# Prologue of a windowed-attention kernel: load order, issuing engine, who makes the weights' high parts, and when a slab is measured

## The reference

```python
g = v.reshape(B, H, W, 32, 12)                     # group norm: 32 groups of 12 channels
xn = (g - mean(g, (1, 2, 4))) / sqrt(var(g) + eps) # statistics over a whole image
x_ = roll(xn, (-3, -3), axis=(1, 2))
q, k, v = split(x_ @ w_qkv.T, 3)                   # 12 heads of 32, windows of 7 x 7 tokens
dots = q @ k.T * 32**-0.5 + pos_emb[rel] + mask    # 49 x 49 for each window and head
out = softmax(dots) @ v
y = x + roll(out @ w_out.T + b_out, (3, 3), axis=(1, 2))
```

## Time and profile before

| | |
|---|---|
| median of 3 runs | 4351.02 us |
| the profiled execution | 4347.23 us, its span 4345.4 us |
| TensorE (PE) busy | 4176.7 us, 96% |
| VectorE (DVE) busy | 3730.7 us, 86% |
| ScalarE (ACT) busy | 2266.6 us, 52% |
| GpSimd (POOL) busy | 2231.0 us, 51% |

### The profile page before, as it was taken

The page is one execution under the profiler, slowest core; times in us unless marked ns, Lnnn a source line. Parts: engine busy times, 40 slices in busy tenths (PEclk is TensorE's granted clock), DMA queues, the critical chain, the costliest instruction groups (busy, mean ns, idle before and its releaser), DMA issues.

```text
span 4345.4 us, 166334 instructions
## 1 busy us (share of the span) xinstructions
PE 4176.7 (96%) x65384; PEld 2993.6 (69%) x65384; DVE 3730.7 (86%) x9283; ACT 2266.6 (52%) x4225; POOL 2231.0 (51%) x1933
## 2 busy tenths in 40 slices
PE   3999999999999999999999999999999999999998
PEld 1677767677776767767677677767767777676776
DVE  5888888988888888888888888888888888888887
ACT  0555555555555555555555555555555555555554
POOL 1455555555554555555555555555555555455554
PEclk9999999999999999999999999999999999999999
DMA  4345444444444443444444444444534444444442
GB/s 125 101 109 126 104 110 118 107 113 111 114 114 103 110 122 102 111 121 107 111 115 111 112 112 108 119 108 106 123 101 111 125 103 112 113 113 112 101 105 61
DMA packets 231108, 479.07 MB, mean 110 GB/s; under 512 B 39009, under 2 KB 140898, under 8 KB 222818
## 3 DMA queue, kind: packets, MB, share of 16 engines
q1 hardware_dynamic: 230338, 468.43, 42.5%
HBM read 159.99 MB, written 77.07 MB: 55 GB/s over the span
## 4 chain that ended last, share of the span: by engine, by line
PE 52%; DVE 23%; SPq 9%; ACT 7%; issue 4%; DMA 4%; DVEq 0%; POOL 0%; ACTq 0%; POOLq 0%
PE ps_pj L1100 14%; PE ps_post L1196 11%; PE ps_pj L1096 10%; SPq L466 6%; DVE st L714 5%; ACT ph L681 5%; DMA stack<-qk 4%; DVE mx L924 3%; PE ps_post L1187 3%; DVE lg L913 3%; PE ps_sa L1134 2%; PE ps_st L1164 2%; DVE qk L878 2%; PE ps_pv L1180 2%; ACT qk L607 2%
## 5 line engine op out<-in xcount | busy, mean ns | idle before, releaser
L575 POOL TENSOR_TENSOR rb<-tq,cst 128x588 bf16<-128x588 bf16 x512 | 606.4, 1184 | 1723.8 <-ACT tq L668 1723.8
L607 ACT ACTIVATE qk<-ps_pj 128x392 f16<-128x392 f32 x768 | 382.0, 497 | 927.3 <-PE ps_pj L1100 921.0
L681 ACT ACTIVATE ph<-ps_st,sc 64x588 f16<-64x588 f32 x1024 | 772.2, 754 | 6.5
L1100 PE MATMUL ps_pj<-xh,wh 128*128 128x392 f16 x2304 | 766.6, 333 | 6.7 <-POOL xl L539 3.9
L1100 PE MATMUL ps_pj<-xh,wl 128*128 128x392 f16 x2304 | 765.8, 332 | 0.0
L1100 PE MATMUL ps_pj<-xl,wh 128*128 128x392 f16 x2304 | 765.5, 332 | 0.0
L878 DVE TENSOR_TENSOR qk<-ps_pj,qk 128x392 f16<-128x392 f32 x768 | 432.2, 563 | 377.7 <-ACT qk L607 373.4
L561 POOL TENSOR_TENSOR pl<-pf,ph 64x588 f16<-64x588 f32 x512 | 649.8, 1269 | 149.4 <-POOL rb L575 120.4
L547 POOL TENSOR_TENSOR xb<-xs,bout 98x384 f32<-98x384 f32 x512 | 518.3, 1013 | 119.3 <-DMA out<-xb 99.2
L966 DVE TENSOR_TENSOR pl<-pf,ph 64x588 f16<-64x588 f32 x512 | 533.2, 1041 | 0.0
L1178 PE MATMUL ps_pv<-vh,ph 128*128 128x33 f16 x6144 | 516.3, 177 | 1.2 <-DVE pl L966 1.2
(11 more groups left out here) (107 smaller groups left out, 8887.0 us busy)
## 6 DMA issues: line engine op xcount, KB each, us to landing
stack<-qk SPq DMA_DIRECT2D x1536, 147.0 KB
sx<-in_x SPq DMA_DIRECT2D x66, 1176.0 KB, 11.6
xs<-in_x SPq DMA_DIRECT2D x384, 84.0 KB
out<-xb SPq DMA_DIRECT2D x384, 84.0 KB
xs<-in_x SPq DMA_DIRECT2D x384, 63.0 KB
out<-xb SPq DMA_DIRECT2D x384, 63.0 KB
xs<-in_x SPq DMA_DIRECT2D x128, 66.0 KB
out<-xb SPq DMA_DIRECT2D x128, 66.0 KB
```

The source lines that it names most:

```text
L575: nc.gpsimd.tensor_tensor(rb[:, :, :, :], tq[:, :, :].unsqueeze(2).broadcast_to([128, 2, HH, N]), const_of("own_head").unsqueeze(1).unsque ...
L681: e = nc.scalar.activation(ph[rows, :, w * PAD:w * PAD + N].rearrange("p (a h) n -> p a h n", a=2), ps_st[rows, :, 0:HH * N].rearrange("p ...
L1100: m = mm(ps_pj[bank][:, 0:RT].rearrange("p (w n) -> p w n", w=NW), wa[:, c, o:o + 128], xa[:, b, c, :, 0:N], **on)
```

## The change

The slabs' loads go first on SyncE and the constants' behind the weights'. The positions and the x rows are issued from ScalarE's stream. ScalarE makes the high parts of the weights (an activation with copy and scale), VectorE keeps the low parts. VectorE measures slab 0 and 1 ahead of the maxima, and slab 0 of image 1 behind the units of the first row.

```diff
         @block.sync
         def _(sp):
-            sp.dma_start(cst[:, :], const[:, :]).then_inc(s_const, 16)
-            sp.dma_start(wnat[:, :, :], ...).then_inc(s_const, 16)
-            sp.dma_start(wonat[:, :, :], ...).then_inc(s_const, 16)
-            sp.dma_start(brow[:, :], ...).then_inc(s_const, 16)
             slab(0, 0, 0)
             slab(0, 1, 1)
-            sp.wait_ge(s_init, 1)
-            (14 loads of bn from pos, then_inc(s_const, 16))
-            load_row(Tick(0, 0), 0)
-            load_row(Tick(0, 0), 1)
+            sp.dma_start(wnat[:, :, :], ...).then_inc(s_const, 16)
+            sp.dma_start(wonat[:, :, :], ...).then_inc(s_const, 16)
+            sp.dma_start(cst[:, :], const[:, :]).then_inc(s_const, 16)
+            sp.dma_start(brow[:, :], ...).then_inc(s_const, 16)
             for s in range(2, SLABS):
                 sp.wait_ge(s_bn, s - 1)
                 slab(0, s, s % 2)
             sp.wait_ge(s_bn, SLABS - 1)
             slab(1, 0, 0)
             sp.wait_ge(s_bn, SLABS + 1)
             slab(1, 1, 0)
         @block.scalar
         def _(act):
+            act.wait_ge(s_init, 1)
+            (the same 14 loads of bn, act.dma_start)
+            for odd in range(2):
+                at = rows_of(Tick(0, 0), odd)
+                for p in range(PAIRS):
+                    move_row(act, x, xs[:, odd, p, :], s_load[odd], p, True, at)
+            act.wait_ge(s_pre, SC_MADE)
+            u = 0
+            for kind in ("w", "o"):
+                for c in range(KC):
+                    for a in range(3 if kind == "w" else 1):
+                        act.wait_ge(s_pj, u + 1)
+                        nc.scalar.activation(hi_[:, c, a * C:(a + 1) * C], ps_pj[u % 2][:, 0:C], ACT.Copy,
+                                             scale=s).then_inc(s_cast, 1)
+                        u += 1
         @block.vector
-            dve.wait_ge(s_slab[0], 16)
-            measure(0, range(GROUPS), True)
+            for s in range(2):
+                dve.wait_ge(s_slab[s], 16)
+                measure(s, range(GROUPS), True, s)
             dve.wait_ge(s_const, 16 * (4 + 2 * WS))
 ...
-                        dve.wait_ge(s_pj, u + 1)
-                        nc.vector.tensor_scalar(hi_[:, c, cols], ps_pj[u % 2][:, 0:C], s, None, ALU.mult).then_inc(s_cast, 1)
                         dve.wait_ge(s_cast, u + 1)
 ...
-            for s in range(1, SLABS):
+            for s in range(2, SLABS):
                 dve.wait_ge(s_slab[s % 2], 16 * (s // 2 + 1))
                 measure(s, range(GROUPS), True, s % 2)
 ...
-            dve.wait_ge(s_slab[0], 16 * 3)
-            measure(0, range(GROUPS), True)
             dve.wait_ge(s_fz, FZ)
 ...
             assert u == PRO_UNITS
+            dve.wait_ge(s_slab[0], 16 * 3)
+            measure(0, range(GROUPS), True)
```

More of the change, by code:

```diff
@@ L421, in _ @@
         def _(sp):
-            sp.dma_start(cst[:, :], const[:, :]).then_inc(s_const, 16)
-            sp.dma_start(wnat[:, :, :], w_qkv.rearrange("(a p) c -> p a c", p=128)).then_inc(s_const, 16)
-            sp.dma_start(wonat[:, :, :], w_out.rearrange("(a p) c -> p a c", p=128)).then_inc(s_const, 16)
-            sp.dma_start(brow[:, :], b_out.rearrange("(a c) -> a c", a=1)).then_inc(s_const, 16)
             def slab(img, s, b):
@@ L430, in _ @@
             slab(0, 1, 1)
-            sp.wait_ge(s_init, 1)
[L433 to L442, removed]
-            load_row(Tick(0, 0), 0)
-            load_row(Tick(0, 0), 1)
+            sp.dma_start(wnat[:, :, :], w_qkv.rearrange("(a p) c -> p a c", p=128)).then_inc(s_const, 16)
+            sp.dma_start(wonat[:, :, :], w_out.rearrange("(a p) c -> p a c", p=128)).then_inc(s_const, 16)
+            sp.dma_start(cst[:, :], const[:, :]).then_inc(s_const, 16)
+            sp.dma_start(brow[:, :], b_out.rearrange("(a c) -> a c", a=1)).then_inc(s_const, 16)
             for s in range(2, SLABS):
@@ L598, in _ @@
         def _(act):
+            act.wait_ge(s_init, 1)
+            row = 2 * WS - 1
+            for r in range(WS):
+                windows = bass.AP(pos.tensor, r * row, [[1, WS], [row, WS], [1, WS]])
+                for at in (0, 64):
+                    q = at + r * WS
+                    act.dma_start(bn[q:q + WS, :].rearrange("p (r c) -> p r c", r=WS), windows).then_inc(s_const, 16)
+            for odd in range(2):
[7 more added lines that the diff above has]
+                    for a in range(3 if kind == "w" else 1):
+                        hi_ = wh if kind == "w" else woh
+                        s = sg[:, 0:1] if kind == "w" else sg[:, 1:2]
+                        act.wait_ge(s_pj, u + 1)
+                        nc.scalar.activation(hi_[:, c, a * C:(a + 1) * C], ps_pj[u % 2][:, 0:C], ACT.Copy,
+                                             scale=s).then_inc(s_cast, 1)
+                        u += 1
             def high(unit, kind, i, b, p_free, stack_sem, stack_need, bank):
```

## The result

The change makes the kernel slower: 4365.12 us (median of 8 runs, 4362.91 to 4369.27) against 4350.87 us for the kernel before (8 runs, 4347.77 to 4355.9). The ratio is 1.0033, with a 95% interval of 1.0022 to 1.0044, or 9.6 to 19.1 us. The forecast was no change, 4352.2 us, with a range that ended at 4361. The profiled execution has a span of 4361.5 us.

The account below looks back on a forecast made before the run. The prediction took the first score matmul's start, when `stack` is ready, as the bound; -16.0 + 13.6 + 3.2 + 0.4 = +1.2 us made 4348.4 profiled, 4352.2 us as median, range 4343 to 4361.

Parts of the forecast that it names:

- Rival 2: Slower: ScalarE still issuing DMAs when the scalars are made; each 0.1 us more per issue costs 3.4 us; 4364 us; chance 8%.
- rival 3: Loads land late and the slab delays the stack fully: +5.6 us, 4356.6 us; chance 15%.
- Rival 1: SyncE's wait does not set the start of the scores, so the whole 16 us arrive: 4335 us; chance 5%.
- (a): Reordered loads: weights, constants and positions finish landing earlier, -1.5 us, between -3.8 and +0.5.
- (d): VectorE's measurements and ScalarE's table load leave the path between cast and first projection: -6.3, -4.7 and -1.3 us.
- (b): 34 DMA issues moved from SyncE to ScalarE ahead of its casting: cost 0, covered by 1.1 us or more.
- (c): Weight casts shared by ScalarE and VectorE: last low part 2.2 us earlier, bounds -3.0 and -1.0.
- (e): SyncE's in-order program: the stack loads queue behind its wait for the moved measurement, +13.6 us.
- (f): The slab issued just ahead of the stack in the same rings delays the stack's landing: +3.2 us, from 0 to 3.8.
- (g): TensorE idles about 20 us before the first scores, then runs longer at half pace: +0.4 us, between 0 and 1.

Follow-up runs that it names:

- e0: The kernel before, unchanged, run again to see what two equal kernels differ by; ratio 1.0001 to the kernel before.
- e3: The changed kernel with the measurement of image 1's first slab back ahead of the normalisation of x; ratio 1.0000 to the kernel before.
- e4: The kernel before with only image 1's first slab measured after the units of the first row; ratio 1.0034 to the kernel before.
- e11: The kernel before with image 1's first slab measured after the first three tiles of x, where VectorE idled; ratio 0.9992 to the kernel before.
- e6: The changed kernel with SyncE holding slab 2 of image 0 until the first maximum is made; ratio 1.0009 to the kernel before.
- e2: The changed kernel with ScalarE issuing the 20 x-row loads after the 12 high parts of the weights; ratio 1.0013 to the kernel before.
- e9: e8 with slab 2 of image 0 also held until the first maximum; ratio 0.9971 to the kernel before.
- e1: The changed kernel with the first row's 12 stack loads issued ahead of SyncE's wait and image 1's second slab; ratio 0.9992 to the kernel before.
- e10: The changed kernel with image 1's second slab issued behind the 12 stack loads, SyncE's wait kept; ratio 1.0016 to the kernel before.
- e8: The changed kernel with x rows issued after the high parts and image 1's first slab measured after three x tiles; ratio 0.9974 to the kernel before.
- e5: The changed kernel with both x rows issued after the high parts and the stack ahead of SyncE's wait; ratio 0.9989 to the kernel before.

## Why the prediction was wrong, step by step

The way of reading held: the first scores decide, and they hang on the stack. The sum to them was +0.8 us (+1.2 less the half speed after them); the profile has +10.3, or +12.1 against e0. Rivals 2 and 3, given 8% and 15% as alternatives, came true together: ScalarE was still issuing, the tables landed late and the slab delayed the stack fully. Rival 2's own price of 3.4 us for each 0.1 us gives 7.5 us for 1.13 an issue; 5.0 were lost. Rival 1 is out: the measurement's place sets the start (e3, e4). By the prediction's own steps:

- **(a) failed.** Forecast -1.5, ends -3.8 and +0.5; measured +1.3 (24.30 to 25.63). The pair flatters it: four kernels with the old loads (before, e0, e4, e11) have 23.23 to 24.30, four with the new ones 25.63 to 25.98, +2.0 between the means. I charged the 1.2 MB of x rows to it, but not slab 2: that its issue moves from 35 to 12 us stands only in (d), as a gain. Holding it back brought the tables 2.0 us sooner (e6), taking the x rows away 1.2 (e2), both together 3.2 (e9, 22.44).
- **(b) failed, the largest miss.** Cost 0 was forecast, with ScalarE free at 22 to 31 us. It was free at 39.36. The trip point of rival 2 was 0.91 us an issue, the measured mean 1.13. I had read SyncE's stalls as a matter of its own bulk ("while the rings were full", which no row shows; the rows show the stalls, and a DMA share of 1.0) and let ScalarE off with "cover 1.1 us or more"; a cover of 1 us over an unmeasured 30 us chain of issues in the busiest 30 us of the DMA engines deserved far more than 8%. With tables and stall taken apart, it cost 5.0 us (e2). The pace itself was not wrong: with slab 2 held back (e6) ScalarE is free at 30.4, for 30.7 forecast. So 7.0 of the 9.5 us missed, all of (b) and 2.0 of (a), come back when one load of 1.2 MB, which the change itself brought forward, is held back.
- **(c) held within its bounds.** From the first low part to the last took 12.4 us (41.35 to 53.74), 12.0 forecast; from tables landed, e2 took 1.9 us less than the kernel before, -2.2 forecast.
- **(d) held.** From the last low part to the first projection: 36.2 us before, 24.0 after, -12.2 against -12.3 forecast. Slab 2 and 3 were there, and no wait stood between them (the row at 55.90).
- **(e) held to 0.1 us.** From the last `vl` to the stack's issue: -8.45 before, +5.20 after; +13.65 for +13.6. e1, e3 and e4 show the cause from three sides.
- **(f) was mis-sized.** 15.0 us from issue to scores for 10.7: +4.3 for +3.2, above its end of 3.8 (e10 gives 4.2).
- **(g)** (+0.4 forecast) cannot be told from noise: from the first scores to those of the next step it is 7.2 us, 7.4 before, but 8.6 in e0, the same kernel.

Added up: -7.7 to the first projection, where -16.0 was forecast, +13.65, +4.3. That is +10.3. The misses of (a), (b) and (f) are 2.8 + 5.0 + 1.1 = 8.9 of the 9.5 us; the rest is 0.4 of (c), the cast loop being that much longer than counted, and rounding. The forecast's +13.6 of (e) and -12.3 of (d) were right for the reasons given. All differences against one profile of the kernel before carry the 2 us of e0. One slip in the prediction does not change this: rival 3's +5.6 needs the bad end of (c) too, (a), (f) and (g) alone give +4.4.

The rule of the Trainium skill that I weighed at (a) (DMA: Bandwidth & Descriptors, "Issuing engines are not separate DMA queues": engines interleave, and issuing from a second one saves issue time only) pointed the right way, and I gave it too little: here the second queue did not even save issue time (38.4 us for 34 issues, 29.8 on SyncE before). Its other section on this, "Queues, rings and completion order" of the same page, says that a DMA engine goes round between the rings packet by packet. From 18 to 23 us the queues of SyncE (q1) and ScalarE (q10) moved, in packets, MB and share:

```profile
DMA packets 237, 1.52 MB, mean 304 GB/s; under 512 B 31, under 2 KB 83, under 8 KB 83
q1 hardware_dynamic: 185, 1.46, 102.0%
q10 hardware_dynamic: 52, 0.06, 4.3%
```

ScalarE had one packet in 4.6, but its packets average 1.2 KB against 7.9, so it moved 4% of the bytes. By packets the rule would allow it half of them; the row shows fewer, and nothing here tells whether that is the rings or ScalarE's own supply. Packets of 1.2 KB beside packets of 7.9 KB, and so few bytes for ScalarE's queue, is what the rows show and what I left out. That the size of the other queue's packets is the cause fits them, but no run varied it.

## What to carry to other kernels

When a call is moved along one engine, look at every semaphore it raises and read the program of each engine that waits for it from that wait downwards: here a measurement taken off VectorE's chain held back twelve unrelated loads on SyncE, and 4.7 us saved cost 18 (13.65 of (e), 4.3 of (f)). When a load is brought forward, ask what lands later for it, also in other queues. Do not put a queue's issues ahead of work on a compute engine while another queue keeps the DMA engines full; issue on it only what is needed first, and the rest after the work. A gap of known length on the same engine, here 5.5 us for 4.8, is the place for work that nobody waits for yet, and it must be ahead of the last point at which somebody does.

## What the runs showed of the hardware that was not expected

- One DMA issue on ScalarE's queue can block the engine for 11 us (10.99, against a median of 0.81 for the same 20 issues, and 0.67 to 0.85 for all 20 in e2, where the DMA engines' share was 0.19 and then, with one slab beside them, 0.69).
- A load issued in the same queue behind others can still delay them: slab 2, issued at 12.28, after the last of SyncE's table loads was issued at 9.38, put off the landing of the tables by 2.0 us (e6), and by 1.7 without the x rows beside it (e8 against e9).
- ScalarE's table load ran as soon as a weight tile was in PSUM (25.45), while the activation behind it still waited for VectorE until 33.46 (e2). In this run it had waited for TensorE alone, and not for all that its activation waits for; e5, e8 and e9 show the same, the load 1.0 us after the tables each time.
- TensorE ran the 24 first score matmuls in 0.73 us in the changed kernel, after 21.3 us of idle, and in 0.49 in the kernel before, after 3.4. The length of that idle alone does not decide it: e0 and e5 took 0.72 us after 3.4 us of idle, e3 and e8 0.49 and 0.50 after 3.4. In the changed kernel the granted clock was 0.50, the lower of the two levels, already while TensorE idled, here from 104 to 113 us:

```profile
104.00:113.00 9.00, 0.00 (x0) 0.00 (x0) 1.41 (x10) 0.00 (x0) 0.00 (x0) 0.50 0.74 189
```
